# FFN attention: the maxima's split and turning moved to other places of the turn, and the turns written out

## The reference

```python
x = x + 0.5 * ffn(layernorm(x))
x = x + linear_attention(layernorm(x))
x = x + 0.5 * ffn(layernorm(x))

# in ffn:
scores = einsum('bhsk,bhtk->bhst', Q[..., :8], K) / sqrt(8)
attn = softmax(scores, axis=-1)          # row maximum taken off, exp, normalised
ao = einsum('bhst,bhtv->bhsv', attn, V)
mla_out = concat([ao, 0]) @ o_w + o_b
probs = softmax(mla_out @ router_w + router_b); top 2 of 8 experts; gelu MLP of each
```

## Time and profile before

| what | value |
|---|---|
| median of 3 runs | 2490.47 us (2488.42 to 2494.25) |
| the profiled execution's own time | 2496.27 us |
| its span, first to last instruction | 2494.6 us |
| mean granted TensorE clock | 0.875 of full |
| TensorE, VectorE, ScalarE, GpSimd busy | 79%, 62%, 38%, 26% of the span |

### The profile page before, as it was taken

How to read it: one execution, slowest core, us unless ns; L and a number is a source line. 1 busy time by engine, 2 the same in 40 slices (tenths; PEclk the granted TensorE clock), 3 DMA queues, 4 the chain that set the end, 5 groups by cost and what they waited for, 6 DMA issues and landing times. The chain is left out here.

```text
span 2494.6 us, 43922 instructions
## 1 busy us (share of the span) xinstructions
PE 1965.2 (79%) x12512; PEld 1086.7 (44%) x12513; DVE 1541.0 (62%) x3524; ACT 938.1 (38%) x1694; POOL 656.6 (26%) x674
## 2 busy tenths in 40 slices
PE   3898988898289959888889874599989898369940
PEld 2323333332079945655656563123333332069940
DVE  3688878885244436656666663588878885244433
ACT  1056556567122214322333321046555567212210
POOL 7422333221312231111100004522332321312246
PEclk9799999999689978888897886589998999779975
DMA  4333323220122231111011001332323230032236
GB/s 123 58 62 57 62 54 61 51 49 11 68 98 73 73 129 35 52 52 53 18 40 47 27 18 34 71 63 56 62 55 59 48 57 11 26 131 73 70 116 189
DMA packets 154273, 155.20 MB, mean 62 GB/s; under 512 B 19744, under 2 KB 144416, under 8 KB 153760
## 3 DMA queue, kind: packets, MB, share of 16 engines
q1 hardware_dynamic: 122912, 108.39, 19.1%
q0 software_dynamic: 10752, 26.23, 3.4%
q10 hardware_dynamic: 20448, 18.62, 2.1%
HBM read 90.80 MB, written 62.39 MB: 61 GB/s over the span
## 5 line engine op out<-in xcount | busy, mean ns | idle before, releaser
L501 DVE TENSOR_REDUCE f_M<-bank 128x1 f32<-128x512 f32 x1024 | 666.6, 684 | 222.1 <-PE bank L749 201.9
L435 ACT ACTIVATE f_PT<-bank 128x512 f32<-128x512 f32 x1024 | 574.9, 596 | 341.2 <-PE bank L768 330.7
L749 PE MATMUL bank<-f_KS,f_QS 96*128 96x512 bf16 x1024 | 424.8, 417 | 111.0 <-DVE f_M L501 79.3
L768 PE MATMUL bank<-f_QS,f_KS 99*128 99x512 bf16 x1024 | 402.5, 397 | 29.6 <-ACT f_PT L435 21.9
L778 PE MATMUL bank<-f_PT,f_V 128*32 128x512 f32 x2048 | 282.7, 627 | 0.0
L768 PEld LDWEIGHTS bank<-f_QS,f_KS 99*128 99x128 bf16 x1024 | 101.1, 100 | 395.6 <-ACT f_PT L435 268.3
L749 PEld LDWEIGHTS bank<-f_KS,f_QS 96*128 96x128 bf16 x1024 | 103.1, 101 | 262.7 <-DVE f_M L501 186.7
L1064 PE MATMUL bank<-f_w,f1m_gT 128*128 x568 | 136.2, 383 | 0.1
L1064 PE MATMUL bank<-f_w,f2m_gT 128*128 x568 | 135.9, 382 | 0.1
L357 POOL DMA_INDIRECT routed_rows<-f_AO,f_rows_i x128 | 124.2, 970 | 42.1 <-issue 42.1
L331 POOL TENSOR_TENSOR f_xr<-f_hs,f_half 128x1024 f32<-128x1024 f32 x16 | 30.3, 1893 | 301.7 <-DVE f_hs L81 268.8
(11 more groups left out here) (279 smaller groups left out, 3272.1 us busy)
## 6 DMA issues: line engine op xcount, KB each, us to landing
f_QS<-q_parts SPq DMA_DIRECT2D x192, 64.0 KB
f_KS<-k_parts SPq DMA_DIRECT2D x192, 64.0 KB
expert_rows<-f1m_y ACTq DMA_DIRECT2D x71, 128.0 KB, 1.7
expert_rows<-f2m_y ACTq DMA_DIRECT2D x71, 128.0 KB, 1.7
xr<-f_xr SPq DMA_DIRECT2D x16, 512.0 KB, 3.0
f_w<-in_L_ffn_w SPq DMA_DIRECT2D x4, 2048.0 KB, 8.2
q_parts<-f_q SPq DMA_DIRECT2D x16, 384.0 KB, 2.5
k_parts<-f_k SPq DMA_DIRECT2D x16, 384.0 KB, 2.5
```

The costliest lines, as they stand in the source:

```text
L435: act.activation(PT[:, i % 8, :], SCE[i % 2][:, :], ACT.Exp).then_inc(probs_ready, 1)
L501: dve.tensor_reduce(M[:, t, h:h + 1], SCM[n % 3][:, :], AX.X, ALU.max).then_inc(scm_drained, 1)
L749: pe.matmul(SCM[n % 3][:, :], QS[par][0:K_MAX, h, t * P:(t + 1) * P], KS[par][0:K_MAX, h, :], start=True, stop=True).then_inc(scm_filled, 1)
L768: pe.matmul(SCE[i % 2][:, :], KS[par][0:K_EXP, h, t * P:(t + 1) * P], QS[par][0:K_EXP, h, :], start=True, stop=True).then_inc(sce_filled, 1)
```

## The change

- `run_turns` has no hardware loop: all turns are written out.
- The split of the maxima is issued one instruction after each tile instead of all four at once. The first half (batch s) is split in group 12, turned after group 13 and copied after the first tile of group 14 of the same turn. The second half is split in group 0 of the next turn (where the batch is e), turned after group 3 and copied in group 4.
- The turned maxima go to bank SIDE[1] instead of an SCM bank, so the three SCM banks hold scores only; the copy signals a semaphore of its own, mT_ready, and the other users of SIDE[1] wait for it.
- On SP `maxima(e, 1)` now stands first in the turn; `maxima(s, 0)` stands where it stood, ahead of `stack_half(f, 0)`; the order is `maxima(e, 1)`, XR, X, q and k parts, `maxima(s, 0)`, `stack_half(f, 0)`, `stack_half(f, 1)`.

```diff
--- before.py
+++ after.py
...
-    A_FRONT, A_SCM, A_POST = LN_STEPS, 3 * HALVES, 2 + 22
-    PER_UNIT = SC + HALVES
+    G_LAST, G_FIRST = 0, 12
+    A_FRONT, A_SCM, A_POST = LN_STEPS, 3, 2 + 22
...
@@ run_turns
-            full = B - 3
-            with eng.Fori(0, full // 2) as k:
-                for odd in range(2):
-                    b = k * 2 + (START + 1 + odd)
-                    turn(b, b + 1, b + 2, b - 1, (START + 1 + odd) % 2)
-            for b in range(START + 1 + full // 2 * 2, END + 1):
+            for b in range(START + 1, END + 1):
                 turn(b if b < END else None, b + 1 if b + 1 < END else None,
                      b + 2 if b + 2 < END else None, b - 1)
@@ block.sync: maxima, turn
             def maxima(a, half, par):
-                sp.wait_ge(scm_drained, a * PER_UNIT + max_slot(half) + 1)
+                sp.wait_ge(mT_ready, a * HALVES + half + 1)
                 sp.dma_start(m_scr[half], mT[:, :]).then_inc(m_stored, 16)
...
             def turn(e, s, f, p, par=None):
+                if e is not None:
+                    maxima(e, 1, par_e)
                 if f is not None:
...
                     stack_half(f, 0, par_f, e * SC + SC // 2 if e is not None else None)
-                if s is not None:
-                    maxima(s, 1, par_s)
                 if f is not None:
                     stack_half(f, 1, par_f, (e + 1) * SC if e is not None else None)
@@ block.vector: maximum, split_maxima, evacuate_mT, turn
-                n = score_slot(i)
...
-                dve.tensor_reduce(M[:, t, h:h + 1], SCM[n % 3][:, :], AX.X, ALU.max).then_inc(scm_drained, 1)
+                dve.tensor_reduce(M[:, t, h:h + 1], SCM[(a * SC + i) % 3][:, :], AX.X, ALU.max).then_inc(scm_drained, 1)
...
-            def split_maxima(a, half, s):
+            def split_maxima(a, half, s, n):
                 mh = M[:, :, half * HH:(half + 1) * HH]
-                dve.wait_ge(scm_drained, a * PER_UNIT + score_slot((half + 1) * PER_HALF - 1) + 1)
-                wait(dve, mT_filled, a * HALVES + half)
-                s.own(dve.tensor_scalar(m3[:, :, 0, :], mh, -1.0, None, ALU.mult))
-                s.own(dve.scalar_tensor_tensor(mres[:, :, :], mh, -1.0, m3[:, :, 0, :], ALU.mult, ALU.subtract))
-                s.own(dve.tensor_copy(m3[:, :, 1, :], mres[:, :, :]))
-                dve.tensor_tensor(m3[:, :, 2, :], mres[:, :, :], m3[:, :, 1, :], ALU.subtract).then_inc(m3_ready, 1)
+                if n == 0:
+                    dve.wait_ge(scm_drained, a * SC + (half + 1) * PER_HALF)
+                    wait(dve, mT_filled, a * HALVES + half)
+                    s.own(dve.tensor_scalar(m3[:, :, 0, :], mh, -1.0, None, ALU.mult))
+                if n == 1:
+                    s.own(dve.scalar_tensor_tensor(mres[:, :, :], mh, -1.0, m3[:, :, 0, :], ALU.mult, ALU.subtract))
+                if n == 2:
+                    s.own(dve.tensor_copy(m3[:, :, 1, :], mres[:, :, :]))
+                if n == 3:
+                    dve.tensor_tensor(m3[:, :, 2, :], mres[:, :, :], m3[:, :, 1, :], ALU.subtract).then_inc(m3_ready, 1)
...
-                dve.tensor_copy(mT[:, :], SCM[max_slot(half) % 3].bitcast(BF16)[0:PARTS * HH, 0:S]).then_inc(scm_drained, 1)
+                dve.tensor_copy(mT[:, :], SIDE[1].bitcast(BF16)[0:PARTS * HH, 0:S]).then_inc(mT_ready, 1)
...
-                    if s is not None:
-                        if g == HH:
+                        if e is not None and g == G_LAST:
+                            split_maxima(e, 1, s_last, i % HQ)
+                        if s is not None and g == G_FIRST:
+                            split_maxima(s, 0, s_scm, i % HQ)
+                        if e is not None and g == G_LAST + 4 and i % HQ == 1:
+                            evacuate_mT(e, 1)
+                        if s is not None and g == G_FIRST + 2 and i % HQ == 0:
                             evacuate_mT(s, 0)
-                        if g % HH == HH - 1:
-                            split_maxima(s, g // HH, s_scm)
-                if s is not None:
-                    evacuate_mT(s, 1)
@@ block.tensor: turn_hs, project_v, score_for_max, turn_maxima, turn
+                    wait(pe, mT_ready, (a - 1) * HALVES)
...
+                if t == 0:
+                    wait(pe, mT_ready, (a - 1) * HALVES + 1)
...
-                wait(pe, scm_drained, a * PER_UNIT + (n - 2 if n >= 3 else 0))
+                wait(pe, scm_drained, a * SC + i - 2)
...
-                pe.wait_ge(scm_drained, a * PER_UNIT + n - 2)
                 pe.wait_ge(m3_ready, a * HALVES + half + 1)
-                rows = SCM[n % 3].bitcast(BF16)
+                rows = SIDE[1].bitcast(BF16)
...
-                    if s is not None and g == HH:
+                    if e is not None and g == G_LAST + 3:
+                        pe.wait_ge(v_ready, min(e + 2, END) if isinstance(e, int) else e + 2)
+                        if p is not None:
+                            pe.wait_ge(ao_ready, (p + 1) * 2)
+                        turn_maxima(e, 1)
+                    if s is not None and g == G_FIRST + 1:
+                        if p is not None:
+                            pe.wait_ge(logits_ready, p + 1)
                         turn_maxima(s, 0)
...
-                if s is not None:
-                    turn_maxima(s, 1)
```

More of the change, by code:

```diff
@@ L125, in head @@
         return q // 2 * HH + g * 2 + q % 2
[L127 to L133, removed]
     with ExitStack() as ctx:
@@ L186, in attend_and_route @@
         scm_filled, scm_drained = sem("scm_filled"), sem("scm_drained")
-        m3_ready, mT_filled = sem("m3_ready"), sem("mT_filled")
+        m3_ready, mT_filled, mT_ready = sem("m3_ready"), sem("mT_filled"), sem("mT_ready")
         m_stored, m_loaded = sem("m_stored"), [sem(f"m_loaded{half}") for half in range(HALVES)]
@@ L264, in turn @@
             def turn(e, s, f, p, par=None):
-                par_s, par_f = parity(s, 1, par), parity(f, 0, par)
+                par_e, par_s, par_f = parity(e, 0, par), parity(s, 1, par), parity(f, 0, par)
+                if e is not None:
+                    maxima(e, 1, par_e)
                 if f is not None:
@@ L609, in turn @@
             def turn(e, s, f, p, par=None):
-                s_scm = Steps(dve, dve_scm, s, A_SCM) if s is not None else None
+                s_last = Steps(dve, dve_scm, e * HALVES + 1, A_SCM) if e is not None else None
+                s_scm = Steps(dve, dve_scm, s * HALVES, A_SCM) if s is not None else None
                 s_front = Steps(dve, dve_front, f, A_FRONT) if f is not None else None
@@ L622, in turn @@
                             POST[g](p, s_post, i % HQ, parity(p, 1, par))
-                    if s is not None:
-                        if g == HH:
-                            evacuate_mT(s, 0)
-                        if g % HH == HH - 1:
-                            split_maxima(s, g // HH, s_scm)
-                if s is not None:
-                    evacuate_mT(s, 1)
-                for steps in (s_scm, s_front, s_post):
+                        if e is not None and g == G_LAST:
[5 more added lines that the diff above has]
+                        if s is not None and g == G_FIRST + 2 and i % HQ == 0:
+                            evacuate_mT(s, 0)
+                for steps in (s_last, s_scm, s_front, s_post):
                     if steps is not None:
@@ L742, in score_for_max @@
             def score_for_max(a, i, par):
-                n = score_slot(i)
-                if i % (SC // 2) == 0:
-                    pe.wait_ge(half_loaded[i // (SC // 2)], (a + 1) * HALF)
-                wait(pe, scm_drained, a * PER_UNIT + (n - 2 if n >= 3 else 0))
+                if i % PER_HALF == 0:
+                    pe.wait_ge(half_loaded[i // PER_HALF], (a + 1) * HALF)
+                wait(pe, scm_drained, a * SC + i - 2)
                 h, t = i // T, i % T
-                pe.matmul(SCM[n % 3][:, :], QS[par][0:K_MAX, h, t * P:(t + 1) * P], KS[par][0:K_MAX, h, :],
+                pe.matmul(SCM[(a * SC + i) % 3][:, :], QS[par][0:K_MAX, h, t * P:(t + 1) * P], KS[par][0:K_MAX, h, :],
                           start=True, stop=True).then_inc(scm_filled, 1)
             def turn_maxima(a, half):
-                n = max_slot(half)
-                pe.wait_ge(scm_drained, a * PER_UNIT + n - 2)
                 pe.wait_ge(m3_ready, a * HALVES + half + 1)
-                rows = SCM[n % 3].bitcast(BF16)
+                rows = SIDE[1].bitcast(BF16)
                 for t in range(T):
```

## The result

The changed kernel takes 2592.69 us in the median of four runs (2585.24 to 2597.42), against 2492.25 for the kernel before (2488.42 to 2494.25): a ratio of 1.0402, interval 1.0373 to 1.0432. It is slower by 4%, some 100 us. Forecast were 2600 us, 2553 to 2645.

What follows compares the result with a forecast made beforehand. No engine is full over a turn; stalls of TensorE's in-order queue, or of VectorE where full, set it. Lateness +133, clock +18, small instructions +23, split -42 and written-out turns -22 sum to +110: 2600 us, range 2553 to 2645.

Steps and rivals of the forecast that it cites:

- Lateness (+133): At the start of 14 turns, the first maxima matmul waits 9.5 us each for stack loads queued on SP: +133 us.
- The clock after the stall (+18): After TensorE's stop at each turn's start, a low clock costs 1.3 us in 14 turns: +18 us, bounds 0 to +42.
- The mid-turn split (-42): Groups 8 and 9: moving the split away from GpSimd's own split saves 3.0 us in 14 turns: -42 us.
- the four instructions in their new places (+23): Split instructions and copy in groups 0, 4 and 12 cost VectorE time: +23 us, bounds 0 to +35.
- rival 4: Dear split is not GpSimd's doing and stays dear at group 12: 2642 us; chance 0.16 together with rival 3.
- Turns written out (-22): The four looped turns of each phase lose their surplus over the written-out turn: -22 us, bounds 0 to -22.
- rival 3: Scatters and stack share DMA engines and the clock stays at half for four groups: 2645 us; chance 0.16 together with rival 4.
- Rivals 1 and 2: At turn starts: 1, stack not late, 2440 us, chance 0.06; 2, half the lateness won back, 2490 to 2500, chance 0.03.

Runs made afterwards that it cites:

- experiment 1: The changed kernel with stack_half(f, 0) put ahead of maxima(s, 0) on SP's queue, so the stack's loads go first: 2450.66 us, ratio 0.9836.
- 3 to 5: The changed kernel with the first half's split in group 10, 8 or 13 instead of 12: 2499.37, 2474.53 and 2637.34 us.
- 6: The changed kernel with only 6 of the 12 loads for the first stack half of each batch: 2496.01 us, ratio 1.0019.
- experiment 4: The changed kernel with the first half's split in group 8 instead of 12, SP's order as in the changed kernel: 2474.53 us, ratio 0.9932.
- experiment 2: The kernel before with its hardware loop of four turns replaced by written-out turns, nothing else: 2474.52 us, ratio 0.9925.
- experiment 7: The changed kernel with the stack's loads first and the four split instructions issued in one piece after the last tile of groups 0 and 12: 2453.38 us, ratio 0.9853.

## Why the prediction was right, and where its terms were off

The place, the mechanism and the sum held: +110 us were forecast and some +100 measured. The signs that the prediction named came: waits of 9.7 to 11.2 us at the start of fourteen turns, the split's instructions under 0.2 us each, and groups 8 and 9 at 7.57 us. That the sum is so near is in part luck, since a lateness put too low and a clock term put too high cancel. By experiments the change splits into three steps:

| step | from, to (us) | measured | forecast |
|---|---|---|---|
| turns written out | 2490.7, 2474.5 | -16 | -22 |
| split moved, spread and put in its own bank | 2474.5, 2450.7 | -24 | -42 + 23 = -19 |
| the stack's loads behind it in SP's queue | 2450.7, 2592.7 | +142 | +133 + 18 = +151 |

- **Lateness (+133).** Forecast were 17.5 us from the end of tile 56's maximum to the next turn's first maxima matmul. At the end of the turn e = 4, the longest wait of the fourteen, that maximum ends at 489.28, SP's store follows the copy at 489.63 and the matmul starts at 507.83, 18.6 us after the maximum:

```profile
488.00 1.28 DVE L487 TENSOR_REDUCE f_M<-bank 128x1 f32<-128x512 f32 x2
489.20 0.40 DVE L506 COPY f_mT<-bank 24x512 bf16<-24x512 bf16 x1
```

  Store to load takes 1.9 us of it and first stack load to the end of the wait 16.0, where 1.6 and, with the scatters, 15.1 were put. TensorE could have issued that matmul at about 496.5, 0.23 us after the turn's first score as in experiment 1: 7.2 us after the maximum and not 8.0. The forecast says that the turn's end loses some 0.6 us of transposes and waiting, but took its 8.0 with them in. Counted from the turn's first score to its first maxima matmul, the fourteen turns are 148 us longer than in experiment 1, 10.6 each, where 9.5 were put. That the lateness is the queue's order, follows the copy's place and is made of the transfer's length is shown by experiments 1, 3 to 5, and 6.
- **The clock after the stall (+18): the term that was wrong.** The windows view of the turn e = 5 from the end of the wait to the end of group 1, the changed kernel and then experiment 1 without the stall:

```profile
507.83:516.02 8.19, 7.74 (x32) 3.00 (x32) 7.37 (x23) 4.59 (x9) 0.19 (x1) 0.73 0.58 65
```

```profile
447.55:455.50 7.95, 6.30 (x32) 2.08 (x31) 7.36 (x23) 5.43 (x11) 1.92 (x2) 1.00 0.59 80
```

  The clock is at 0.73 after the stall, as expected, and it costs 0.24 us, not 1.3; the rest of the turn takes 55.29 us in both. VectorE is busy 7.4 us of either stretch: where it is the full engine, a slower TensorE hides behind it. That was the prediction's lower bound, and its own row should have decided for it. All ten full turns lose no more than 0.24 us. In the turn e = 6, which has no statistics of a next batch on VectorE, more is lost. From the first maxima matmul to the turn's end, again the changed kernel and then experiment 1:

```profile
581.69:637.68 55.99, 53.51 (x289) 16.40 (x289) 49.93 (x112) 36.12 (x66) 4.72 (x7) 0.95 0.13 20
```

```profile
511.02:565.52 54.50, 51.50 (x290) 15.05 (x288) 49.56 (x112) 36.97 (x68) 6.64 (x9) 1.00 0.14 24
```

  That is 1.5 us, and 1.6 in the second phase. All fourteen together lose some 5 us after the wait, where 18 were put. 148 and 5 are more than the 142 of the table: in experiment 1 the turns before e = 0 are 4.0 and 2.8 us longer (the wait for the turned maxima is one part), and some 3 us stay unaccounted for.
- **The mid-turn split (-42) and the four instructions in their new places (+23).** Together -24 against -19; no run took them apart. The prediction has both halves' maxima beside GpSimd's split, but only the first half's were, once in each of the fourteen turns, so its count stands. Groups 8 and 9 of the turn e = 5, which took 10.09 us:

```profile
540.12:547.69 7.57, 6.44 (x44) 2.62 (x41) 6.54 (x16) 5.08 (x10) 5.21 (x5) 1.00 0.29 104
```

  That is 2.5 us less, not 2.9, and the clock is full where it was at 0.83, so the 2.5 is not the split's alone. GpSimd still meets the logits of batch p there: in group 8 of experiment 1, L530 takes 0.80 us beside it, and 0.19 where it comes a little later, in experiment 4. That the split is cheap at group 12 holds (rival 4 falls), and that GpSimd makes it dear is shown by experiment 4.
- **Turns written out (-22).** Measured -16. The size was read as the difference between turns of one trace, which was some 5 us above the median, and part of it was the clock that a turn happened to get.
- **Scatters beside the stack (rival 3).** The transfer was hardly slowed: from the first issue to the last landing of its twelve loads, the fourteen transfers took 14.6 to 15.9 us, and 14.4 to 15.2 in the kernel before. So the 12 to 14 us that the prediction read from the DMA share are too low, and the 14.6 that it took is right. Its share of 0.58 is also more than the 0.50 that eight engines of sixteen could give; no term rests on it. Rivals 1 and 2 did not come.

## What to carry to other kernels

A DMA queue that is fed in order is part of the schedule: moving a wait later in a turn moves everything issued behind it, and a transfer that was never waited for can become a stall of 10 us in every turn. Before a producer is moved, list what its queue issues after the wait and when each is due; here the cure was to swap two calls, and it turned a loss of 4% into a gain of 1.6%. A small VectorE instruction here cost by its neighbour on GpSimd rather than by its length, so look for a place where GpSimd computes nothing; spreading such instructions out does not help by itself.

## What the runs showed of the hardware that was not expected

**The scatters waited, not the stack.** The views of waits, before and then after, for GpSimd's wait for its row scatters to land (total, times, longest):

```profile
POOL f_pool_carrier L362 <- DMA routed_rows<-f_AO,f_rows_i: 31.4, 16, 3.1
```

```profile
POOL f_pool_carrier L349 <- DMA routed_rows<-f_AO,f_rows_i: 118.8, 16, 11.6
```

In the kernel before and in experiment 2 (35.3 us) the scatters of a turn are issued before the stack's loads (from 254.5 to 263.7 and from 264.5, in the kernel before). In the changed kernel and in experiment 1 (110.4 us) a stack's stream runs beside them, and the wait is three to four times as long, while the first stack half's twelve loads took 14.6 to 15.9 us against 14.4 to 15.2. No cost of the longer wait shows: experiment 1 has it too and is the fastest kernel here, with experiment 7 within the spread.

**The full clock held through all full turns of a run.** In experiment 1 the full turns of both phases show 1.00, against 0.93 to 0.97 before, with the same matmuls. What holds it stays open: VectorE's dear split in mid-turn is gone there, but experiment 2 still has it, and some of its full turns show 1.00 as well.
